# A two-layer transformer program in float32 on one core: the routed feed-forward block makes its queries and keys with the weights stationary, in one float32 product per chunk, and splits only its value and output weights

## The chip, the cores and the metric

The program runs on one core of one Trainium2 chip. The number that counts is the device time of the whole program, in microseconds (us); the median of three runs stands for the kernel. The profile is one more execution, taken by the hardware profiler.

## The reference, cut to what matters

Two layers over 2048 tokens of 512 features. The second layer's feed-forward part is "routed": 256 tokens are chosen by a score, and only these go through a small transformer block of their own. Here `x` holds the chosen tokens, 16 query heads share 8 key heads, and a head has 128 features.

```python
h = _rms_norm(x, ln1_w)
q  = (h @ wq + bq).reshape(S, 16, 128)        # S = 256
kk = (h @ wk + bk).reshape(S, 8, 128)
v  = (h @ wv + bv).reshape(S, 8, 128)
q  = q * cos + _rotate_half(q) * sin          # cos, sin: by the token's position
kk = kk * cos + _rotate_half(kk) * sin
att = softmax(causal(einsum('shd,thd->hst', q, repeat(kk)) / sqrt(128)))
x1 = x + einsum('hst,thd->shd', att, repeat(v)).reshape(S, 2048) @ wo
h2 = _rms_norm(x1, ln2_w)
mlp = silu(h2 @ w_gate) * (h2 @ w_up) @ w_down
```

## The kernel before, in words

The kernel is a chain of stages. Each stage is one block in which every engine has an instruction list of its own; engines meet at semaphores, and a stage begins only when all engines have left the one before. The names: PE is TensorE, DVE VectorE, ACT ScalarE, POOL GpSimd, SP the queue that issues most DMAs. Two stages matter here.

**stage_output1** (L2274) closes the attention of the second layer: 16 tiles of 128 tokens in 4 blocks, `out = r + (o * z) @ w`. For blocks 1 to 3 the DVE multiplies the raw attention output by the inverse sums (`normal`, L2399), ACT rounds the product to the short float format (`high`, L2360), the DVE takes the rest (`low`, L2403), and PE multiplies with three products for each chunk: high by high, high by rest, rest by high (`mm3`, L68 to L76). Such a triple stands for one product of full precision. SP loads the inverse sums `z`; the load for block 3 (`inverses(3)`) stands in SP's list behind residual loads that wait for stores of tiles 0 to 3. In the same stage POOL gathers the chosen tokens and their rows of the cosine and sine tables, and the chosen tokens are normalised, turned by PE (`transposed`) and weighed into `hT`, features by tokens. Beside this, the first 12 pieces of the query, key and value weights (128x512 each, named by `qkv_piece`) are split: ACT makes the high part (L2369), POOL the rest (L2351). At the end ACT and DVE split `hT` into `hTh` and `hTl` (L2380, L2424).

**stage_routed** (L2472) is the block of the reference above. Its first part works in 12 units of 128 tokens by 512 features (4 heads): PE makes the product with the tokens stationary (`product`, 12 matmuls), the DVE adds the bias out of the bank (`biased`, L2891), POOL multiplies by the cosines (`cosines`, L2581), the DVE by the sines in two halves (`sines`, L2901), the DVE adds the two (`turned_sum`, L2909), PE turns the four heads (`transposes`, L2645) and ACT copies them to `qT` or `kT` (L2764). Four units of values follow (L2928). Between these the remaining 20 weight pieces are split by ACT with POOL (L2588) or the DVE (L2914). Then come the scores, softmax and values of each of 16 heads (L2662 to L2688; `spread` is the turning of the probabilities at L2677), with two heads of scores issued ahead. POOL splits the output weights alone, 16 pieces, each a cast (L2604) and a subtraction (L2606). The product with `wo` takes 16 triples for each of 2 token tiles; the gated part follows.

Where a tile lies is given by hand: the weights in one large tensor `WA`, their rest parts written over them (`WAr`), the high parts in four ring buffers, and many later tiles over earlier ones.

Of the kernel before, what the change touches and what calls it, by code (L numbers as in the profile page):

```python
# [17 lines left out]
P = 128  # L18
F32 = mybir.dt.float32
# [2191 lines left out]
class Routed:  # L2211
# [4 lines left out]
    def __init__(self, G, M):  # L2216
# [5 lines left out]
        self.hTl = G.nc.alloc_sbuf_tensor_at("hTl", [P, NC, SEL], F32R, offset=self.hT_at)  # L2222
        self.hTh = G.nc.alloc_sbuf_tensor_at("hTh", [P, NC, SEL], F32R, offset=G.out_o1_at)
# [7 lines left out]
        M.sb("aligned", [P, 24])  # L2231
        self.sq_done, self.ms_done, self.sd_done, self.hn_done, self.hT_mm, self.hT_done, self.ln_in = (
            G.sem("ro_" + n) for n in ("sq", "ms", "sd", "hn", "hT_mm", "hT", "ln_in"))
        self.b_in = [G.sem(f"ro_b_in{k}") for k in range(3)]
        self.kh_done, self.kl_pool, self.kl_dve, self.hTh_done, self.hTl_done = (
            G.sem("ro_" + n) for n in ("kh", "kl_pool", "kl_dve", "hTh", "hTl"))

    def load_bias(self, queue, I, k):
        FQ, FK = NHQ * HDF, NHK * HDF
        a, name, n = ((FQ, "bk", FK), (0, "bq", FQ), (FQ + FK, "bv", FK))[k]  # L2240
        queue.dma_start(self.bias[:, a:a + n], I[name].partition_broadcast(P)).then_inc(self.b_in[k], 16)
# [32 lines left out]
def stage_output1(nc, G, I, S, R, out):  # L2274
# [12 lines left out]
    with ExitStack() as stack:  # L2287
# [15 lines left out]
        def _(sp):  # L2303
# [34 lines left out]
            R.load_bias(sp, I, 0)  # L2338

        @block.gpsimd  # L2340
        def _(pool):
            for m in range(NS):
                where = bass.IndirectOffsetOnAxis(G.idx[:, m:m + 1], 0)
                pool.indirect_dma_start(R.xs[:, m, :], None, S.xn, where).then_inc(gath, 16)
                for n, name in enumerate(("cos128", "sin128")):
                    pool.indirect_dma_start(R.cs[n][:, m, :], None, I[name], where).then_inc(gath, 16)
                pool.indirect_dma_start(R.sc[:, m:m + 1], None, S.score.unsqueeze(1), where).then_inc(gath, 16)
            for p in range(AHEAD * NC):
                whole, hi, low_part = qkv_piece(G, R, p)
                pool.wait_ge(R.kh_done, p + 1)  # L2350
                pool.tensor_tensor(low_part, whole, raw(hi), ALU.subtract).then_inc(R.kl_pool, 1)  # L2351
            pool.wait_ge(gath, 16 * 4 * NS)

        @block.scalar
        def _(act):
# [6 lines left out]
            def qkv_high(p):  # L2362

                if p == 0:
                    act.wait_ge(G.wqkv_in, 48)
                if p == NC:
                    act.wait_ge(o_mm, BT)
                whole, hi, low_part = qkv_piece(G, R, p)
                act.activation(hi, whole, ACT.Copy).then_inc(R.kh_done, 1)  # L2369

            for t in range(NT):
# [5 lines left out]
                elif k == BT - 1:  # L2377
                    for m in range(NS):
                        act.wait_ge(R.hT_done, m + 1)
                        act.activation(R.hTh[:, :, m * P:(m + 1) * P], R.hT[:, :, m * P:(m + 1) * P], ACT.Copy  # L2380
                                       ).then_inc(R.hTh_done, 1)
# [8 lines left out]
        def _(dve):  # L2390
# [30 lines left out]
            for m in range(NS):  # L2421
                dve.wait_ge(R.hTh_done, m + 1)
                cols = slice(m * P, (m + 1) * P)
                dve.tensor_tensor(R.hTl[:, :, cols], R.hT[:, :, cols], raw(R.hTh[:, :, cols]), ALU.subtract  # L2424
                                  ).then_inc(R.hTl_done, 1)
# [31 lines left out]
QU, KU = NHQ * HDF // BANK, NHK * HDF // BANK  # L2457
GROUPS = [("k", u) for u in range(KU)] + [("q", u) for u in range(QU)] + [("v", u) for u in range(KU)]
AHEAD = 3
POOL_LOWS = 26  # L2460


def qkv_piece(G, R, p):

    n, c = divmod(p, NC)
    name, u = GROUPS[n]
    cols = slice(u * BANK, (u + 1) * BANK)
    whole, low = (dict(zip("qkv", routed_qkv(WA)))[name][:, c, cols] for WA in (G.WA, G.WAr))
    return whole, R.ring[n % 4][:, c, :], low


def stage_routed(nc, G, I, R, out):  # L2472


    names = ("qk_mm", "qb", "t1", "s1", "y", "yt_mm", "yt", "v_mm", "v", "link")
    qk_mm, qb_done, t1_done, s1_done, y_done, yt_mm, yt_done, v_mm, v_done, link = (G.sem("ro_" + n) for n in names)
    b_in = R.b_in
# [3 lines left out]
    names = ("woh", "wol", "oh", "ol", "x1t_mm", "hh", "hl", "square", "rs", "guh", "gul", "gu_mm", "sig", "sg", "m", "mt_mm",  # L2481
             "mh", "ml", "wdh", "wdh_act", "wdl", "dn_mm", "dx", "delta", "added")
    (woh_done, wol_done, oh_done, ol_done, x1t_mm, hh_done, hl_done, sq_done, rs_done, guh_done, gul_done, gu_mm, sig_done,
     sg_done, m_done, mt_mm, mh_done, ml_done, wdh_pool, wdh_act, wdl_done, dn_mm, dx_done, delta_done, added) = (
        G.sem("ro_" + n) for n in names)
    wo_in, wgu_in, wd_in = ([G.sem(f"ro_{n}{k}") for k in range(4)] for n in ("wo_in", "wgu_in", "wd_in"))
    FQ, FK = NHQ * HDF, NHK * HDF
# [3 lines left out]
    NU = NS * (KU + QU)  # L2491
    JOBS = FB * NS
    scale = 1.0 / float(np.sqrt(HDF))
    with ExitStack() as stack:
        M = Memory(nc, stack, "ro_")
        WA, WAr = G.WA, G.WAr
        qT = M.far("qT", [P, NHQ, SEL])
# [8 lines left out]
        bias = R.bias  # L2506
        oT = bias[:, :].rearrange("p (h n) -> p h n", h=NHQ)
# [4 lines left out]
        three_at = nc.sbuf_base  # L2512
        qb, t1, y = (M.sb(n, [P, 2, BANK]) for n in ("qb", "t1", "y"))
        nm, ssum, rsum = (M.sb(n, [P, 3, NS]) for n in ("nm", "ssum", "rsum"))
        SB = (0, 1, 6)
        pr, pt = M.sb("pr", [P, 3, 3 * P]), M.sb("pt", [P, 2, 3 * P])
        gate = M.sb("gate", [P, NS])
        at = lambda name, shape, offset: nc.alloc_sbuf_tensor_at("ro_" + name, shape, F32R, offset=offset)
        oTh, oTl = at("oTh", [P, NHQ, SEL], qT_at), at("oTl", [P, NHQ, SEL], R.bias_at)
        mTh, mTl = at("mTh", [P, NF, SEL], qT_at), at("mTl", [P, NF, SEL], R.bias_at)  # L2520
        three = at("three", [P, 6, BANK], three_at)
        hT2h = at("hT2h", [P, NC, SEL], three_at + 2 * 2 * BANK * 4)
        sig, mt = qb, t1
        hTh, hTl = R.hTh, R.hTl
        guA = [at("guA0", [P, NC, BANK], kT_at), at("guA1", [P, NC, BANK], v_at)]
        guB = [at("guB0", [P, NC, BANK], G.out_o1_at), at("guB1", [P, NC, BANK], R.rows_at)]
        spare = [R.hTh, R.hTl]
        wo_high = [guB[1][:, h, :] for h in range(4)] + [guB[0][:, 2 + h, :] for h in range(2)]
        wo_high += [three[:, h, :] for h in range(6)]
        wo_high += [t[:, 2 * h:2 * h + 2, :].rearrange("p c n -> p (c n)") for t in spare for h in range(2)]  # L2530
        wo = [(R.ring32[h // 4][:, h % 4, :], wo_high[h], R.ring[h // 4][:, h % 4, :]) for h in range(NHQ)]

# [6 lines left out]
        def down_piece(f):  # L2539
# [7 lines left out]

        units = [(GROUPS.index((name, u)), name, off, u, m, dst) for name, off, dst, count in (("k", FQ, kT, KU), ("q", 0, qT, QU))
                 for u in range(count) for m in range(NS)]
        vunits = [(GROUPS.index(("v", u)), u, m) for u in range(KU) for m in range(NS)]  # L2550

        @block.sync
        def _(sp):
            R.load_bias(sp, I, 1)
            R.load_bias(sp, I, 2)
            for c in range(4):
                if c < 2:
# [645 lines left out]
```

## Time and profile before

| | |
|---|---|
| median of 3 runs | 1627.05 us (1625.93 to 1630.09) |
| profiled execution, its own time | 1624.44 us |
| its span, first to last instruction | 1622.7 us |
| PE busy | 1499.0 us, 92% |
| DVE, ACT, POOL busy | 1068.6, 770.7, 556.2 us |
| granted clock of TensorE, mean | 0.965 |

The span is 1.74 us shorter than the execution's own time. Matmuls are pipelined, so a matmul's listed duration is longer than the distance to the next one; distances between starts are what adds up. Where a float32 matmul of the program is run, the trace has two records for it, each with a weight load.

### The profile page before, as it was taken

The numbers are of one execution on the slowest core, as the hardware profiler recorded it, in microseconds if no ns is written. First come the engines' busy times: TensorE is split into PE (matmuls) and PEld (weight loads), VectorE is DVE, ScalarE is ACT, GpSimd is POOL, SyncE is SP. The second block draws the span as 40 slices with busy tenths as digits, with TensorE's granted clock in tenths as the row PEclk, the third lists the DMA queues.
The fourth block names the chain that finished last, engine by engine and source line by source line (L and its number), as shares of the span: only waits on it lengthen the run. The fifth ranks groups of instructions, "written<-read, shape, count | busy, mean of one in ns | idle before, by whom it ended". The sixth has DMA issues, their size and how long they took to land. (4 is left out here: it accounts for less than half of the span.)

```text
span 1622.7 us, 23648 instructions
## 1 busy us (share of the span) xinstructions
PE 1499.0 (92%) x7009; PEld 1072.6 (66%) x7009; DVE 1068.6 (66%) x2800; ACT 770.7 (47%) x1311; POOL 556.2 (34%) x752
## 2 busy tenths in 40 slices
PE   5999999999999997899788989999999987887998
PEld 4777888888767886688654545555555545666876
DVE  5453666666567577777567776666667856797583
ACT  5523666656665233333224545555554552333661
POOL 0000677777532333323111212221221224288052
PEclk9999999999999999899959999999999998998999
DMA  5002121221101234466792404314314107706121
GB/s 176 1 1 84 72 107 71 90 87 74 40 27 53 100 109 136 119 192 185 219 291 109 111 8 115 69 54 114 73 48 114 56 25 226 229 31 225 60 104 14
DMA packets 107301, 163.11 MB, mean 101 GB/s; under 512 B 12272, under 2 KB 63616, under 8 KB 100672
## 3 DMA queue, kind: packets, MB, share of 16 engines
q1 hardware_dynamic: 103200, 155.86, 31.6%
q10 hardware_dynamic: 3360, 4.72, 0.8%
q0 software_dynamic: 640, 1.31, 0.4%
q8 instruction: 47, 0.77, 0.2%
q14 instruction: 54, 0.44, 0.1%
HBM read 119.00 MB, written 42.87 MB: 100 GB/s over the span
## 5 line engine op out<-in xcount | busy, mean ns | idle before, releaser
L2042 ACT ACTIVATE l_pt<-banks 128x1024 f32<-128x1024 f32 (+3 forms) x288 | 218.5, 811 | 162.6 <-PE banks L1919 160.7
L2116 DVE CUSTOM_DVE_ANT_0 stage<-banks,l_edges 128x384 f32<-128x384 f32 (+3 forms) x384 | 201.7, 542 | 102.2 <-issue 101.1
L1956 PE MATMUL banks<-l_pt,l_v 128*64 128x512 f32 (+3 forms) x1152 | 230.8, 523 | 3.2 <-POOL l_pt L2014 3.2
L699 POOL TENSOR_TENSOR ex_hl<-ex_h,ex_hh 128x512 fp32r<-128x512 f32 x128 | 165.2, 1296 | 81.3 <-ACT ex_hh L667 81.0
L2013 POOL TENSOR_TENSOR l_turn<-l_before 128x2 f32<-128x2 f32 x192 | 39.4, 205 | 420.1 <-ACT l_pt L2042 410.5
L2119 DVE TENSOR_REDUCE l_mx<-banks 128x1 f32<-128x384 f32 (+1 forms) x208 | 113.2, 544 | 51.0 <-PE banks L1897 50.2
L732 DVE SCALAR_TENSOR_TENSOR ex_rw<-banks,ex_wb 128x512 f32<-128x512 f32 x128 | 88.3, 690 | 78.9 <-PE banks L75 78.8
L1956 PEld LDWEIGHTS banks<-l_pt,l_v 128*64 128x64 f32 x1152 | 70.3, 139 | 95.9 <-issue 71.8
L667 ACT ACTIVATE ex_hh<-ex_h 128x512 fp32r<-128x512 f32 x128 | 80.9, 632 | 103.5 <-DVE ex_h L740 102.8
L1897 PE MATMUL banks<-k,q 96*128 96x384 f32 (+3 forms) x296 | 94.9, 414 | 16.5 <-PEq L3065 8.2
L73 PE MATMUL banks<-ex_xlh,ex_wh 128*128 128x512 f32 x256 | 101.6, 397 | 2.1 <-DVE ex_rw L732 2.1
L74 PE MATMUL banks<-ex_xll,ex_wh 128*128 128x512 f32 x256 | 99.8, 390 | 0.0
L75 PE MATMUL banks<-ex_xlh,ex_wl 128*128 128x512 f32 x256 | 99.8, 390 | 0.0
L1897 PEld LDWEIGHTS banks<-k,q 96*128 96x128 f32 x296 | 54.7, 206 | 68.1 <-issue 24.2
L1897 PE MATMUL banks<-l_k,l_q 96*128 96x384 f32 (+3 forms) x296 | 89.3, 386 | 9.2 <-DVE l_mx L2116 5.5
L1897 PEld LDWEIGHTS banks<-l_k,l_q 96*128 96x128 f32 x296 | 50.6, 193 | 63.1 <-DVE l_mx L2116 26.3
L740 DVE TENSOR_TENSOR ex_h<-banks,ex_t 128x512 f32<-128x512 f32 x128 | 88.4, 691 | 1.1 <-PE banks L75 0.7
L693 POOL TENSOR_TENSOR ex_wl<-ex_ws,ex_wh 128x768 fp32r<-128x768 f32 x16 | 29.6, 1853 | 149.6 <-ACT ex_wh L655 149.6
L2014 POOL TENSOR_SCALAR_AFFINE_SELECT l_pt<-l_pt 128x256 f32<-128x256 f32 x192 | 80.7, 420 | 0.1
L661 ACT ACTIVATE ex_t<-ex_rw 128x512 f32<-128x512 f32 x128 | 79.0, 617 | 1.4 <-DVE ex_rw L732 1.4
L1919 PE MATMUL banks<-q,k 98*128 98x512 f32 (+3 forms) x288 | 68.8, 359 | 1.5 <-ACT q L2061 1.3
L1919 PE MATMUL banks<-l_q,l_k 98*128 98x512 f32 (+3 forms) x288 | 66.4, 349 | 0.7 <-ACT l_pt L2042 0.6
(463 smaller groups left out, 3647.2 us busy)
## 6 DMA issues: line engine op xcount, KB each, us to landing
ex_wb<-gates_by_expert SPq DMA_DIRECT2D x16, 1024.0 KB, 4.6
layer_v<-qkv_vs SPq DMA_DIRECT2D x16, 512.0 KB, 4.7
l_v<-layer_v SPq DMA_DIRECT2D x8, 1024.0 KB, 17.3
layer_qk<-qkv_yh SPq DMA_DIRECT2D x31, 256.0 KB, 3.2
layer_qk<-qkv_yl SPq DMA_DIRECT2D x31, 256.0 KB, 3.6
ex_ws<-ew_in SPq DMA_DIRECT2D x16, 384.0 KB, 5.0
l_q<-layer_qk SPq DMA_DIRECT2D x12, 512.0 KB, 7.7
l_k<-layer_qk SPq DMA_DIRECT2D x12, 512.0 KB, 14.1
```

Of the source, the lines that this page charges most:

```text
L73: pe.matmul(out, ah, bh, start=start and n == 0, stop=False, **kw)
L74: pe.matmul(out, ah, bl, start=False, stop=False, **kw)
L75: last = pe.matmul(out, al, bh, start=False, stop=stop and end, **kw)
L699: pool.tensor_tensor(hl[:, k % RING, :], h[:, k % RING, :], raw(hh[:, k % RING, :]), ALU.subtract).then_inc(hl_done, 1)
L732: dve.scalar_tensor_tensor(rw[:, k % 2, :], gate[k % 2][:, :], 0.0, wb[:, par, b * TB:(b + 1) * TB], ALU.max, ALU.mult).then_inc(rw_done, 1)
L740: dve.tensor_tensor(h[:, k % RING, :], up[k % 2][:, :], tt[:, k % 2, :], ALU.mult).then_inc(h_done, 1)
L1897: pe.matmul(out, q[par][0:K3, h, qt * P:(qt + 1) * P], k[par][0:K3, h, k0 * P:k1 * P], start=True, stop=True).then_inc(a_mm, 1)
L1919: last = pe.matmul(bank[:, 0:width], k[par][0:KM, h, kt * P:(kt + 1) * P], q[par][0:KM, h, qa * P:(qz + 1) * P], start=True, stop=True)
L1956: last = pe.matmul(bank[h * 2 * HD:(h + 1) * 2 * HD, (qa - b * BT) * P:(qz + 1 - b * BT) * P], v[par][:, kt, h, :], pt[:, step_part(b, j), ...
L2042: act.activation(pt[:, step_part(b, j), :, 0:width], G.banks[:, 2 * slot:2 * slot + 2, 0:width], ACT.Exp, scale=scale).then_inc(p_done, 1)
L2116: dve.tensor_tensor_reduce(cutoff[:, n % 4, 0:width], G.ps[5 + n % MB][:, 0:width], masked, 1.0, NEG, ALU.add, ALU.max, mx[:, h, m, c:c + ...
L2119: dve.reduce_max(mx[:, h, m, c:c + 1], G.ps[5 + n % MB][:, 0:width], axis=AX).then_inc(a_red, 1)
```

## The change

- Queries and keys: one matmul per chunk in plain float32, a head's 128x128 weights stationary and all 256 tokens of `hT` moving. Each head lands with features on partitions, as the scores need it; the transposes and their copies go.
- The two tables of the chosen tokens are turned once by PE and copied by ACT (`cosT`, and `sinT` with its halves exchanged).
- The rotary step is done by the DVE out of the bank: three `scalar_tensor_tensor` per head (add the bias of the partition, multiply by the table row), one of 128x256 and two of 64x256; POOL adds the two results in place.
- Weight pieces of queries and keys aren't split any more. The 8 value pieces are split inside the routed stage by ACT and POOL; nothing of this is left in stage_output1. `hT` is split in the routed stage too.
- Four value units stand after 12 of the 24 heads.
- Output weights: ACT makes all 16 high parts after the values; POOL takes rests 0 to 7 between its sums, the DVE rests 8 to 15 within the heads 4 to 11 of the attention.
- SP: `wo` is loaded at the start of the stage, `w_up` after the values, `w_gate` after the last head's product. The query and key biases come as one small tensor.
- After the attention `output_high(0)` and `(1)` stand behind `output(15)`. Several tiles lie elsewhere.

```diff
@@ stage_output1: gone @@
-            R.load_bias(sp, I, 0)
+            R.load_biases(sp, I)
-            for p in range(AHEAD * NC):
-                whole, hi, low_part = qkv_piece(G, R, p)
-                pool.wait_ge(R.kh_done, p + 1)
-                pool.tensor_tensor(low_part, whole, raw(hi), ALU.subtract).then_inc(R.kl_pool, 1)
-                if t < NC:
-                    qkv_high(t)
-                elif t > BT and t - 1 < AHEAD * NC:
-                    qkv_high(t - 1)
-                elif k == BT - 1:
-                    for m in range(NS):
-                        act.wait_ge(R.hT_done, m + 1)
-                        act.activation(R.hTh[:, :, m * P:(m + 1) * P], ...)
...
@@ stage_routed, SP @@
+            for c in range(4):
                 sp.dma_start(R.ring32[c][:, :, :], I["wo"]...).then_inc(wo_in[c], 16)
+            for w, name in ((1, "w_up"), (0, "w_gate")):
+                if w == 1:
+                    sp.wait_ge(v_mm, len(vunits))
+                else:
+                    sp.wait_ge(qk_mm, NH)
...
@@ GpSimd @@
+            def turned_sum(n):
+                dst = head(n)[1]
+                pool.wait_ge(turn_done, n + 1)
+                pool.tensor_tensor(dst, dst, t1[:, n % 3, :], ALU.add).then_inc(y_done, 1)
+            for n in range(NH):
+                turned_sum(n)
+                if n < VALUES_AT and n % 3 < 2:
+                    value_low(2 * (n // 3) + n % 3)
+                if n >= VALUES_AT + 3 and n % 3 < 2:
+                    output_low(2 * ((n - VALUES_AT) // 3 - 1) + n % 3)
+            for h in range(6, 8):
+                output_low(h)
...
@@ TensorE @@
+            def product(n):
+                w, _, h = head(n)
+                wait(pe, turn_done, n - 3)
                 for c in range(NC):
+                    last = pe.matmul(G.ps[n % 4][:, 0:SEL], w[:, c, h * HDF:(h + 1) * HDF], hT[:, c, :], start=c == 0, stop=c == NC - 1)
+                last.then_inc(qk_mm, 1)
+            for k in range(2):
+                for m in range(NS):
+                    last = pe.transpose(G.ps[6 + k][:, m * P:(m + 1) * P], cs[k][:, m, :], G.ident[:, :])
+                last.then_inc(tab_mm, 1)
+            pe.wait_ge(G.wqkv_in, 48)
+            pe.wait_ge(R.hT_done, NS)
+            for n in range(NH):
+                if n == VALUES_AT:
+                    for i in range(len(vunits)):
+                        values(i)
+                product(n)
             def scores(h):
+                if h < 2:
+                    pe.wait_ge(turn_done, NH)
+                    pe.wait_ge(tab_done, 3)
+                pe.wait_ge(y_done, NHK + h + 1)
...
@@ VectorE @@
+            def turned(n):
+                _, dst, _ = head(n)
+                part = G.ps[n % 4][:, 0:SEL]
                 dve.wait_ge(qk_mm, n + 1)
+                wait(dve, y_done, n - 2)
+                dve.scalar_tensor_tensor(t1[:, n % 3, :], part, R.hb[:, n:n + 1], cosT[:, :], ALU.add, ALU.mult)
                 for k in range(2):
+                    rows = slice((1 - k) * P // 2, (2 - k) * P // 2)
+                    last = dve.scalar_tensor_tensor(dst[k * P // 2:(k + 1) * P // 2, :], part[rows, :], R.hb[rows, n:n + 1],
+                                                    sinT[rows, :], ALU.add, ALU.mult)
+                last.then_inc(turn_done, 1)
                 if h + 2 < NHQ:
                     maxima(h + 2)
+                if 4 <= h < 12:
+                    weight_low(h + 4)
```

## Rows read from the trace of the kernel before

**Rows 1.** Windows: stretches in us, busy time (count) by engine, clock, DMA share, GB/s.

```profile
1415.20:1481.60 66.40, 54.17 (x240) 41.00 (x240) 57.05 (x58) 18.82 (x33) 53.44 (x40) 0.97 0.21 72
1481.60:1519.30 37.70, 33.70 (x208) 28.11 (x209) 28.43 (x98) 27.56 (x99) 17.98 (x19) 0.91 0.69 252
1519.30:1622.70 103.40, 94.28 (x424) 75.82 (x424) 59.10 (x82) 43.05 (x80) 33.60 (x26) 0.98 0.15 46
```

**Rows 2.** Waits, 1414 to 1482 us: total, times, longest.

```profile
PE banks L2645 <- DVE ro_y L2909: 11.3, 10, 3.1
```

**Rows 3.** Groups by line, 1414 to 1482 us: busy us, mean ns, idle.

```profile
L2588 POOL TENSOR_TENSOR WAr<-WA,ringr 128x512 fp32r<-128x512 f32 x14 | 20.7, 1492 | 0.0
```

**Rows 4.** Single lines: duration min/median/max in ns, first and last start.

```profile
L2891 DVE TENSOR_TENSOR ro_qb<-banks,bias x12: 676/678/692, 1418.3 to 1465.2; 128x512 f32<-128x512 f32 x12
...
L2901 DVE TENSOR_TENSOR ro_y<-ro_qb,routed_sin x24: 410/1504/1524, 1419.0 to 1467.8; 128x256 f32<-128x256 f32 x24
```

**Rows 5.** Timeline of stage_output1: start, duration, instruction, idle time before it.

```profile
1389.69 0.69 DVE L2399 TENSOR_TENSOR o_o<-o_z,o_o 128x512 f32<-128x512 f32 x1 [3.41 <-DMA o_z<-layer_inverse_sums]
...
1391.64 1.30 POOL L2351 TENSOR_TENSOR WAr<-WA,ringr 128x512 fp32r<-128x512 f32 x1 [4.22 <-ACT ringr L2369]
1391.69 1.80 DVE L2399 TENSOR_TENSOR o_o<-o_z,o_o 128x512 f32<-128x512 f32 x1
...
1401.13 0.80 PE L73 MATMUL banks<-out_wh,o_oh 128*128 128x512 f32 x1 [2.12 <-DVE o_ol L2403]
...
1402.15 0.63 PE L75 MATMUL banks<-out_wh,o_ol 128*128 128x512 f32 x1
1402.57 0.63 PE L73 MATMUL banks<-out_wh,o_oh 128*128 128x512 f32 x1
```

**Rows 6.** The same view, where the two stages meet.

```profile
1412.43 0.40 PE L75 MATMUL banks<-out_wh,o_ol 128*128 128x512 f32 x1
...
1413.47 1.28 DVE L2424 TENSOR_TENSOR hTl<-hT,hTh 128x512 fp32r<-128x512 f32 x2
1413.59 0.34 ACTq L2387 DMA_DIRECT2D out<-rows  x1
...
1415.22 0.47 PE L73 MATMUL banks<-ringr,hTh 128*128 128x512 f32 x1 [2.40 <-PEq L2287]
```

**Rows 7.** Timeline of PE: a value unit's last 9 products.

```profile
1478.50 0.40 PE L73 MATMUL banks<-ringr,hTh 128*128 128x512 f32 x1
...
1480.38 0.39 PE L75 MATMUL banks<-ringr,hTl 128*128 128x512 f32 x1
```

**Rows 8.** The chain that ended last, in time order, 1493 to 1515 us: start, us.

```profile
1495.72 0.43 PE banks L2686 x2
...
1502.51 0.49 PE banks L2667 x2
```

**Rows 9.** Timeline: DVE and POOL together, then 16 chained DVE subtractions.

```profile
1562.52 1.09 POOL L2614 CAST WAr<-ringf 128x512 fp32r<-128x512 f32 x1
1563.06 0.74 DVE L2984 SCALAR_TENSOR_TENSOR ro_qb<-banks,rs,ro_qb 128x512 f32<-128x512 f32 x1
...
1518.74 5.68 DVE L2951 TENSOR_TENSOR ro_oTl<-bias,ro_oTh 128x256 fp32r<-128x256 f32 x16 [2.01 <-ACT ro_oTh L2802]
```

**Rows 10.** Timeline of the attention: PE's turnings of probabilities, and DVE's pace.

```profile
1487.31 0.90 PE L2677 MATMUL banks<-ident,ro_pr 128*128 128x128 f32 x3 [2.86 <-DVE ro_pr L2946]
...
1497.20 0.55 PE L2677 MATMUL banks<-ident,ro_pr 128*128 128x128 f32 x3
...
1508.41 0.50 PE L2677 MATMUL banks<-ident,ro_pr 128*128 128x128 f32 x3
...
1510.23 0.54 PE L2677 MATMUL banks<-ident,ro_pr 128*128 128x128 f32 x3
...
1485.12 1.27 DVE L2939 TENSOR_SCALAR ro_nm<-ro_nm 128x2 f32<-128x2 f32 x1
...
1508.62 0.62 DVE L2935 TENSOR_REDUCE ro_nm<-banks 128x1 f32<-128x128 f32 x2 [0.30 <-PE banks L2669]
```

More of the change, by code:

```diff
@@ L2420, in _ @@
                     low(b + 1, k)
[L2421 to L2425, printed above, removed]
         @block.tensor
@@ L2533, in gu_piece, with head @@
+        def head(n):
+            name, h = HEADS[n]
+            return (wk, kT[:, h, :], h) if name == "k" else (wq, qT[:, h, :], h)
         def gu_piece(fb, n):
@@ L2641, in transposes @@
-            def transposes(n):
-                pe.wait_ge(y_done, n + 1)
-                wait(pe, yt_done, n - 1)
-                for j in range(HB):
-                    last = pe.transpose(G.ps[2 + n % 2][:, j * P:(j + 1) * P], y[:, n % 2, j * P:(j + 1) * P], G.ident[:, :])
-                last.then_inc(yt_mm, 1)
-            for n, (g, name, off, u, m, dst) in enumerate(units):
-                if n < NS:
-                    pe.wait_ge(R.hTl_done, m + 1)
-                wait(pe, qb_done, n - 1)
-                product(G.ps[n % 2], g, m).then_inc(qk_mm, 1)
-                if n >= 2:
-                    transposes(n - 2)
@@ L2655, in _, with values @@
-            for n, (g, u, m) in enumerate(vunits):
-                wait(pe, v_done, n - 1)
-                product(G.ps[4 + n % 2], g, m).then_inc(v_mm, 1)
-                if n < 2:
-                    transposes(NU - 2 + n)
+                    last = pe.matmul(G.ps[n % 4][:, 0:SEL], w[:, c, h * HDF:(h + 1) * HDF], hT[:, c, :], start=c == 0, stop=c == NC - 1)
+                last.then_inc(qk_mm, 1)
+            def values(n):
+                u, m = vunits[n]
+                rows = slice(m * P, (m + 1) * P)
+                wait(pe, v_done, n - 1)
+                if n == 0:
+                    pe.wait_ge(hTl_done, NS)
+                for c in range(NC):
+                    if m == 0:
+                        pe.wait_ge(vwl_done, u * NC + c + 1)
+                    _, hi, low = value_piece(u * NC + c)
+                    last = mm3(pe, G.ps[4 + n % 2], [((hTh[:, c, rows], hTl[:, c, rows]), (hi, low))], start=c == 0, stop=c == NC - 1)
+                last.then_inc(v_mm, 1)
@@ L2707, in _ @@
                     rows = slice(m * P, (m + 1) * P)
-                    last = mm3(pe, G.ps[m], [((oTh[:, h, rows], oTl[:, h, rows]), (hi, low))], start=h == 0, stop=h == NHQ - 1)
+                    last = mm3(pe, G.ps[m], [((oTh[h // 8][:, h % 8, rows], oTl[:, h, rows]), (hi, low))],
+                               start=h == 0, stop=h == NHQ - 1)
                     if h == NHQ - 1:
@@ L2745, in down @@
                     _, hi, low = down_piece(f)
-                    last = mm3(pe, G.ps[4 + m], [((mTh[:, f, rows], mTl[:, f, rows]), (hi, low))], start=f == 0, stop=f == NF - 1)
+                    last = mm3(pe, G.ps[4 + m], [((mTh[:, f, rows], mTl[f // 8][:, f % 8, rows]), (hi, low))], start=f == 0, stop=f == NF - 1)
                 return last
@@ L2811, in _ @@
                     output(h - 1)
-            output_high(0)
-            output_high(1)
             output(NHQ - 1)
-            for h in range(2, NHQ):
+            for h in range(NHQ):
                 output_high(h)
@@ L2931, in maxima, with weight_low @@
+            def weight_low(h):
+                whole, hi, low = wo[h]
+                dve.wait_ge(woh_done, h + 1)
+                dve.tensor_tensor(low, whole, raw(hi), ALU.subtract).then_inc(wol_dve, 1)
             def maxima(h):
```

274 lines of the change are left out of this document (101 added, 173 removed).

## The prediction

> **What bounds the kernel now.** I read the page first: 1622.7 us of span with PE busy for 92% of it, so most of the program is PE's. The change touches three stretches, and I cut the end of the span at them [rows 1]. In the first part of the routed stage (66.40 us) PE is busy for 54.17 us, but the DVE for 57.05 and POOL for 53.44: three engines share the limit. The waits name the holder: PE sits idle for 11.3 us before the transposes of L2645, each time until the DVE's sum is there [rows 2]. The DVE's line in [rows 4] shows the pace: twelve units from 1418.3 to 1465.2 us, so 46.9 / 11 = 4.26 us a unit, while PE's own work in a unit is 12 products at 0.235 us (1480.38 - 1478.50 = 1.88 us over eight distances [rows 7]) = 2.82 us, and four transposes at about 0.13 us (0.50 us for three, ends included [rows 10]). What makes the DVE slow is the sine step: of 128x256 elements, it takes 0.41 us at best and 1.50 us in the median [rows 4]. It reads two SBUF tensors while POOL works.
>
> The same collision stands in the stage before. There `normal` takes 0.69 us when POOL is idle, and 1.80 us when POOL's subtraction of 1.30 us has begun 0.05 us earlier [rows 5]. Three of the four groups of block 3 have it, one of them in the rows (3 times 1.1 us), and PE waits on this chain: 2.12 us before the block's last group at 1401.13 us, after which products come 0.42 us apart (1402.57 - 1402.15), the distance at TensorE's lower level of 1.2 GHz [rows 5].
>
> So the questions are: what float32 products cost PE, whether the DVE and POOL keep up, and what the earlier stage gives back.
>
> **The change, part by part.** Sums are made on the profiled execution.
>
> *A, stage_output1.* The 12 splits leave. The split pieces themselves weren't waited for; they lock the DVE. In block 3, three collisions of 1.80 - 0.69 = 1.11 us go: 3.3 us. With the last wait about 1 us shorter the clock need not drop: 8 products at 0.42 instead of 0.235 us, 1.5 us. The end of the block: PE's last product starts at 1412.43 us and ends its chain near 1412.83, the next stage's first starts at 1415.22, with the split of `hT` between (1413.47, 1.28 us) [rows 6]. Without it the block ends with the addition (about 0.7 us), a store issue (0.34 us) and the meeting of the engines (1415.22 - 1414.75 = 0.47 us): 1.5 instead of 2.4 us, 0.9 us gained. Blocks 1 and 2 lose five collisions too, but block 3 starts on the landing of its inverse sums (the DVE idle for 3.41 us until the DMA [rows 5]). That load stands behind stores which the first chain sets, so it can start up to 3.3 us earlier, or not, where the DMA queues are full. I count 0 for it. A = 5.7 us; bounds 0.9 (the DMA sets everything) and 9.
>
> *B, queries, keys, values.* PE: 24 heads of 4 float32 matmuls. The nearest row is the product with the values, of the same shape, two records of 128x256 in 0.43 us; the score product takes 0.49, where it stands next to bfloat16 masks [rows 8]. Here like follows like, so I take 0.43: 96 x 0.43 = 41.3 us (at 0.49: 47.0). That its rests vanish is why PE gains nothing: before, the same was 12 x (2.82 + 0.52) = 40.1 us. The values are unchanged: 48 x 0.235 = 11.3 us. The table transposes: 4, about 0.6 us. The stage then ends with a rotary step, of which nothing lies beside PE work: three DVE operations.
>
> What do those cost? Not shown before for this size. From above: 0.74 us, the same operation and kinds of operand with 512 elements, and that while POOL's cast (1562.52 to 1563.61) ran beside it: it wasn't locked out. From below: 5.68 / 16 = 0.355 us, a two-input operation of 256 elements in a chain [rows 9]. I take 0.40, nearest to the lower one, since the length is the same: 1.2 us a head against PE's 1.72. At 0.74 it would be 2.22, and the DVE would set the pace (24 x 2.22 = 53.3 us, 12 us more). The 64-partition halves are counted as whole ones.
>
> POOL: per three heads, three additions of 256 elements and two rests. A rest takes 1.30 us alone [rows 5], 1.49 beside others [rows 3]; the addition lies between about 0.4 (a third of that) and 1.3; by half the length and a fixed part I take 0.75. That is 3 x 0.75 + 2 x 1.3 = 4.9 us against 5.2 on PE: it just keeps up, and a lag of two heads is allowed by the three buffers. At 1.3 it would be 6.5 us for three, up to 8 us over the stage. ACT has two tables, `hT`, 8 and then 16 high parts, under 20 us in 53. The start: tables, `hT` split and first rotary step take about 5 us, while PE can fill four banks (7 us): hidden. Without those banks it would cost 3.
>
> B: before 66.4; after 0.6 + 41.3 + 11.3 + 1.5 (last rotary step and its signals) = 54.7. Gain 11.7; bounds 6.0 (0.49) and 0 (DVE at 0.74) below, 12.5 above.
>
> *C, attention.* POOL was busy with `wo` for 17.98 of 37.7 us [rows 1]. The scaling of two numbers took 1.27 us at 1485.12, and PE waited 2.86 us for its first turning at 1487.31; then at low clock and beside POOL the next four heads took 1497.20 - 1487.31 = 9.89 us, where two late ones are 1.82 apart [rows 10]. With POOL done early: the first turning about 1.5 us sooner, and four heads at 1.83 = 7.3, 2.6 us saved. Against it: the DVE gets 8 rests, one a head, some 0.6 us each in a chain. A late head has 0.30 us of DVE idle time [rows 10], so each costs 0.3: 8 x 0.3 = 2.4 us. `output_high(0)` now stands behind the last `output`: 0.65 us before PE's first product with `wo`. POOL's last two rests reach 3 us into the attention; half a microsecond is in the first term. C = 1.5 + 2.6 - 2.4 - 0.65 = 1.0 us; from -3 (clock still drops) to +3.
>
> *D, the loads.* `wo` (4 MB) now lands at the stage's start, where the queues carry 72 GB/s [rows 1] and its first reader comes after the values. `w_up` and `w_gate` come earlier than before; their first reader is behind the attention. The two bias loads stand at the end of SP's list in the stage before, with some 5 us to land. All nothing, hidden by 21 us of products at least. If the weights came late, gate-up would wait, but it has 35 us. After the attention (103.4 us, PE busy for 94.28 [rows 1]) the order of work is the same: 0.
>
> Sum: 5.7 + 11.7 + 1.0 = 18.4 us. Span 1622.7 - 18.4 = 1604.3, own time 1606.0. The profiled execution is 2.6 us below the median of the three runs, so for the median: 1627.05 - 18.4 = 1608.6 us.
>
> **The rivals.**
>
> *R1, the stage before gives nothing.* The DMA queues set block 3 and its stores. For it: [rows 5]'s wait for the inverse sums. Against: after its landing eleven more microseconds pass in which the DVE is busy for nearly all and PE waits for it. Gain 0.9 + 11.7 + 1.0 = 13.6: 1613.5 us. Chance 0.15.
>
> *R2, PE isn't the bound of the new products, or they are dearer.* Products at 0.49 us give 1614.3; DVE operations at 0.74 give 1620.3; a lagging POOL lies between. For: POOL's margin is 6%. Chance 0.17, centre 1615.
>
> *R3, slower: the lock hits the rotary step.* The new operation reads the bank, an SBUF table and an SBUF bias scalar. If the lock took it too, it would wait out POOL's work, up to 4.9 / 3 = 1.6 us a head: 1.2 + 1.6 = 2.8 us, 24 x 2.8 = 67 us instead of 41, 26 us lost: 1634.6 us. It decides from 1.72 + 18.4 / 24 = 2.5 us a head on. Against it: the row with the same kinds of operand, 0.74 us beside POOL's cast [rows 9], and L2891, never above 0.69 us beside POOL [rows 4]. Chance 0.04.
>
> The Trainium skill (SBUF — State Buffer, section "SBUF: two separate sides") says that the port pair is an exclusive lock: a DVE operation with two SBUF inputs and a GpSimd operation block each other for a whole instruction. By that rule the 1.80 us are explained, and the trace agrees (0.69 alone, 1.30 for POOL's); whether a scalar counts as the second input it doesn't say there. If it did, the time would be R3's.
>
> *R4, no change:* the gain of B is eaten by a wait I don't see. Chance 0.04.
>
> **How the numbers follow.** My forecast (1602 to 1612 us) has 0.60. With R1 and R2 the gain runs from 6 to 25 us; leaving out R3 and R4 and the outer tails of R2, the range is 1601 to 1619 us. About 0.3% (5 us) is what a measurement of this kernel tells from no change. R1, R2 and the forecast are all faster by more: 0.92. Within 0.3%: 0.04. Slower: 0.04.
>
> **What would show it.** Score products should begin some 17 us earlier than 1481.6 us. The routed stage's first product: at 1409.5 us. `normal` in block 3: four times 0.69 us. Float32 records in heads: pairs every 0.43 us, no idle time on PE from first product to last; if PE waits on the rotary step, R2 or R3. DVE operations of 0.4 to 0.5 us; above 1 us means R3. POOL's additions at 0.75 us. In the attention, heads 5 to 12 at 2.1 us apart and the others at 1.83. The prediction is wrong if the float32 products run apart by more than 0.5 us, or the clock drops within them, or block 3's inverse sums land later.

## The result and the profile after

The changed kernel took 1606.28 us (median of 4 runs, 1604.26 to 1607.17) against 1626.88 us of the kernel before (4 runs, 1625.93 to 1630.09): a ratio of 0.9868, 95% interval 0.9851 to 0.9885, so faster by 20.6 us. Predicted were 1608.6 us within 1601 to 1619. Run again later, it gave 1606.40 us and 0.9882 (0.986 to 0.9904). The profiled execution took 1604.26 us with a span of 1602.6: 20.1 us less than the 1622.7 before.

The same windows as in [rows 1], with the end of stage_output1 ahead of them (stretch in us, its length, busy time and count of PE, PEld, DVE, ACT and POOL, granted clock, DMA share, GB/s):

```profile
1352.58:1407.71 55.13, 49.86 (x201) 38.82 (x201) 31.30 (x49) 9.07 (x14) 7.86 (x8) 0.93 0.85 269
1407.71:1462.32 54.61, 52.99 (x245) 45.80 (x245) 38.77 (x78) 16.16 (x30) 33.04 (x37) 1.00 0.46 160
1462.32:1498.93 36.61, 32.00 (x209) 25.96 (x209) 28.17 (x106) 27.04 (x100) 3.51 (x4) 1.00 0.31 115
1498.93:1602.60 103.67, 94.00 (x424) 75.82 (x424) 58.90 (x82) 42.78 (x80) 33.71 (x26) 0.98 0.16 46
```

Against [rows 1], the routed stage's first part is 66.40 - 54.61 = 11.8 us shorter, the attention 37.70 - 36.61 = 1.1, the rest 0.3 longer. What remains, 7.5 us, was gained ahead of it: the routed stage begins at 1407.71 us instead of 1415.22. In the first part PE is now busy for all but 1.62 us, the wait at its end, at the full clock of 2.4 GHz. By busy time no other engine is near it (the DVE 38.77 of 54.61 us), but within the heads the DVE is closer than that, as the rows below and kernels 10 and 11 show.

Groups of that part (busy us, mean ns of one | idle time before them and what ended it):

```profile
L2591 PE MATMUL banks<-hT,WA 128*128 128x256 f32 x192 | 41.8, 379 | 0.0
L2856 DVE SCALAR_TENSOR_TENSOR ro_qT<-banks,hb,ro_sinT 64x256 f32<-64x256 f32 x32 | 15.5, 483 | 0.5
L2853 DVE SCALAR_TENSOR_TENSOR ro_t<-banks,hb,ro_cosT 128x256 f32<-128x256 f32 x24 | 11.6, 483 | 5.4 <-PE banks L2591 5.2
L2544 POOL TENSOR_TENSOR ro_qT<-ro_qT,ro_t 128x256 f32<-128x256 f32 x15 | 11.0, 732 | 16.3 <-DVE ro_qT L2856 16.3
```

PE never stands idle before a product of the heads. The DVE's idle time before the cosine step was ended by PE, and POOL's by the DVE: a pipeline with PE in front. The timeline of the DVE (start, duration, instruction, idle time before it) shows two of the 24 heads:

```profile
1457.28 0.48 DVE L2853 SCALAR_TENSOR_TENSOR ro_t<-banks,hb,ro_cosT 128x256 f32<-128x256 f32 x1 [0.25 <-PE banks L2591]
1457.78 0.98 DVE L2856 SCALAR_TENSOR_TENSOR ro_qT<-banks,hb,ro_sinT 64x256 f32<-64x256 f32 x2
1459.01 0.48 DVE L2853 SCALAR_TENSOR_TENSOR ro_t<-banks,hb,ro_cosT 128x256 f32<-128x256 f32 x1 [0.25 <-PE banks L2591]
1459.51 0.98 DVE L2856 SCALAR_TENSOR_TENSOR ro_qT<-banks,hb,ro_sinT 64x256 f32<-64x256 f32 x2
```

A head takes 1459.01 - 1457.28 = 1.73 us, four pairs of records at 0.43. The DVE's three operations of 0.48 us fill 1.48 us of it with the gaps between them, and it waits 0.25 us for the next bank.

Block 3 in stage_output1, to be held against [rows 5], and the junction, against [rows 6]:

```profile
1387.13 0.69 DVE L2372 TENSOR_TENSOR o_o<-o_z,o_o 128x512 f32<-128x512 f32 x1 [3.19 <-DMA o_z<-layer_inverse_sums]
1388.66 0.69 DVE L2391 TENSOR_TENSOR rows<-banks,rows 128x512 f32<-128x512 f32 x1 [0.84 <-DMA rows<-layer_residual]
...
1393.86 0.69 DVE L2372 TENSOR_TENSOR o_o<-o_z,o_o 128x512 f32<-128x512 f32 x1
...
1395.99 0.50 PE L73 MATMUL banks<-out_wh,o_oh 128*128 128x512 f32 x1 [0.63 <-DVE o_ol L2376]
...
1405.74 0.40 PE L75 MATMUL banks<-out_wh,o_ol 128*128 128x512 f32 x1
...
1407.71 0.41 PE L2609 MATMUL banks<-ident,routed_cos 128*128 128x128 f32 x2 [1.57 <-PEq L2282]
```

All twelve `normal` operations of the stage take 0.68 to 0.69 us. From block 3's first one to PE's last group it is 1395.99 - 1387.13 = 8.86 us (11.44 before), from there to the last product 9.75 (11.30 before), and over the junction 1.97 (2.79 before): 2.58 + 1.55 + 0.82 = 4.95 us. The other 2.56 us of the 7.5 were there already: block 3's inverse sums had been used at 1389.69 us before, now at 1387.13.

### The profile page after: what moved, and what is told of

Its sections match the earlier page's. It is cut to its first block and busy times, and to the rows that moved or that the text cites. A ratio compares the mean times of both kernels' runs of the same rounds, so it can differ in the third digit from the quotient of the medians.

```text
span 1602.6 us, 23599 instructions
## 1 busy us (share of the span) xinstructions
PE 1492.9 (93%) x7013; PEld 1072.9 (67%) x7013; DVE 1038.3 (65%) x2826; ACT 759.8 (47%) x1294; POOL 505.4 (32%) x722
## 5 line engine op out<-in xcount | busy, mean ns | idle before, releaser
L1897 PE MATMUL banks<-k,q 96*128 96x384 f32 (+3 forms) x296 | 94.9, 414 | 16.6 <-PEq L3019 8.3
```

The source lines that it names most:

```text
L1897: pe.matmul(out, q[par][0:K3, h, qt * P:(qt + 1) * P], k[par][0:K3, h, k0 * P:k1 * P], start=True, stop=True).then_inc(a_mm, 1)
```

## The experiments

Each kernel ran beside the kernel before on the same chip: before took 1624.97 us beside kernels 1 to 4, 1626.11 beside 5, 6, 7 and 9, and 1623.69 beside 8, 10, 11 and the second run of 6. The changed kernel itself ran beside the second group alone (kernel 5), so the others are held against it by their ratios. Since the landing of a load shifts a whole execution by some microseconds, I read stretches of the trace too: **S**, from the first product of stage_output1, behind a wait of 3.48 us in every profile, to the table transposes (before, where these don't exist, to the routed stage's first product: 1415.22 - 1352.37 = 62.85 us; changed kernel 55.13 and, in its second profile, 55.53), and **T**, from the transposes to the first product with `wo` (91.22 and 91.24 us in the changed kernel).

**1. The splits back in stage_output1 (e1_pool_back).** To the changed kernel the 12 old splits are added in place; their results aren't used.

```diff
+            for p in range(12):
+                whole, hi = old_piece(p)
+                pool.wait_ge(x_hi, p + 1)
+                pool.tensor_tensor(hi, whole, raw(hi), ALU.subtract).then_inc(x_lo, 1)
...
+                if t < NC:
+                    old_high(t)
+                elif t > BT and t - 1 < 12:
+                    old_high(t - 1)
```

> The changed kernel with the twelve splits of the stage before put back in their old places: ACT makes the high parts, POOL subtracts, in place over the high part; nothing reads the result, the weights themselves stay as they are. Theory (the stage before gained because POOL's subtractions no longer lock the DVE): the multiplication by the inverse sums takes about 1.8 us again in three groups of block 3, PE's wait before the last group comes back, and the time is 5 to 7 us above the changed kernel's, 1611 to 1613 us. Rival (the gain comes from the split of hT leaving the end of the stage, or from the DMA): 0 to 1 us above.

Measured: 1610.17 us, 0.9906 (0.989 to 0.9922). By the ratios that is 4 to 6 us above the changed kernel. S is 62.46 us, about 7 more; T is 91.21. The collision is back in the timeline:

```profile
1391.11 1.44 POOL L2354 TENSOR_TENSOR ringr<-WA,ringr 128x512 fp32r<-128x512 f32 x1 [3.91 <-ACT ringr L2371]
1391.31 1.80 DVE L2396 TENSOR_TENSOR o_o<-o_z,o_o 128x512 f32<-128x512 f32 x1
```

The DVE's operation starts 0.20 us after POOL's and takes 1.80 us. All three collisions of block 3 are back (1.80, 1.81, 1.80 us), and with them PE's wait of 2.14 us before the last group and the products 0.42 us apart behind it: 11.33 us from there to the last product, as in the kernel before (11.30).

**2. ACT's half of them alone (e2_act_only).** As 1, without POOL's subtractions.

```diff
-            for p in range(12):
-                whole, hi = old_piece(p)
-                pool.wait_ge(x_hi, p + 1)
-                pool.tensor_tensor(hi, whole, raw(hi), ALU.subtract).then_inc(x_lo, 1)
```

> The same with only ACT's twelve high parts put back, none of POOL's subtractions. Theory (the lock): nothing changes in the DVE's multiplications, 0.69 us each; ACT's 0.6 us a piece stand behind the high part that PE needs, so 0 to 1 us above the changed kernel, 1606 to 1607 us. Rival (ACT's queue was what PE waited for): most of the 5 to 7 us come back here already.

Measured: 1605.07 us, 0.9881 (0.9862 to 0.99), S 55.51, T 91.21: no different from the changed kernel. ACT's copies cost this stage nothing. The stage's gain comes from POOL's subtractions, but for the 0.82 us at the junction, which kernel 1 keeps (1.97 us there too).

**3. The rotary step from SBUF (e3_turn_from_sbuf).** ACT copies each head out of its bank into a buffer of three, and the same three DVE operations read that; ACT's splits are strewn between the copies.

```diff
-                part = G.ps[n % 4][:, 0:SEL]
-                dve.wait_ge(qk_mm, n + 1)
+                part = qc[:, n % 3, :]
+                dve.wait_ge(qc_done, n + 1)
```

> The changed kernel, but ACT copies each head out of the bank to SBUF and the rotary step reads the copy, so that its three operations have two SBUF tensors and an SBUF scalar. ACT's value and output splits are spread between the copies. Theory (the forecast's: what kept the rotary step out of the lock was that it reads the bank): operations of 0.5 us alone but above 1 us beside POOL, a head takes about 1.3 us of DVE and up to 1.6 us of POOL one after the other, 2.9 us, and the part with the 24 heads grows from 54.6 to 75 to 82 us, 1626 to 1634 us in all. Rival (the lock doesn't matter for operations this short): the heads stay at 1.73 us and the time at 1606 to 1608 us.

Measured: 1626.22 us, 1.0008 (0.9995 to 1.0022): the whole gain is gone. The groups of its first part (columns as above), and its window:

```profile
L2865 DVE SCALAR_TENSOR_TENSOR ro_qT<-ro_qc,hb,ro_sinT 64x256 f32<-64x256 f32 x32 | 27.0, 842 | 0.5
L2547 POOL TENSOR_TENSOR ro_qT<-ro_qT,ro_t 128x256 f32<-128x256 f32 x15 | 13.3, 885 | 21.5 <-DVE ro_qT L2865 21.5
```

```profile
1406.56:1478.70 72.14, 56.37 (x244) 46.21 (x245) 60.51 (x78) 25.12 (x54) 41.23 (x37) 0.95 0.45 159
```

With both inputs in SBUF the sine halves rise from 483 to 842 ns in the mean, and POOL's additions from 732 to 885. Two rivals are a slower read from SBUF as such, and a DVE that waits for ACT's copies. The DVE's first two pairs of sine halves, and what POOL does beside the second, speak against the first:

```profile
1410.59 0.97 DVE L2865 SCALAR_TENSOR_TENSOR ro_kT<-ro_qc,hb,ro_sinT 64x256 f32<-64x256 f32 x2
1412.09 2.26 DVE L2865 SCALAR_TENSOR_TENSOR ro_kT<-ro_qc,hb,ro_sinT 64x256 f32<-64x256 f32 x2
...
1411.65 1.01 POOL L2547 TENSOR_TENSOR ro_kT<-ro_kT,ro_t 128x256 f32<-128x256 f32 x1 [49.95 <-DVE ro_kT L2865]
1412.62 1.45 POOL L2552 TENSOR_TENSOR WAr<-WA,ro_guB 128x512 fp32r<-128x512 f32 x1
```

Before POOL begins, the pair takes 0.97 us, against 0.98 from the bank; beside POOL's addition and rest it takes 2.26. And the DVE waited for ACT's copies for 1.7 us in all. Without the transposes (0.46 us) and the values (about 11.3, in part at the lower clock) some 60 us are left for 24 heads, 2.5 us a head: the point which R3 named as the one where the gain is gone. The heads with both of POOL's operations beside them take 2.8 us, those with the addition alone 1.9. So the lock is real for the rotary step too, and what keeps the changed kernel out of it is that the large operand comes from a bank. The Trainium skill (SBUF — State Buffer, section "SBUF: two separate sides") says that a DVE operation with two SBUF inputs and a GpSimd one that reads SBUF exclude each other, and leaves open whether a scalar read from SBUF is such an input. By the 483 ns beside a POOL that is busy for 33.04 of 54.61 us it is not; with the 0.97 and 2.26 us above the trace agrees with the rule.

**4. The rests of `wo` late (e4_rests_late).** The DVE's eight rests stand behind the 16 `output_low` instead of one in each of heads 4 to 11.

```diff
-                if 4 <= h < 12:
-                    weight_low(h + 4)
...
+            for h in range(8, NHQ):
+                weight_low(h)
```

> The changed kernel with the DVE's eight rests of the output weights taken out of the attention and put behind the sixteen subtractions that follow it. Theory (in the heads with a rest the DVE sets the pace at 2.13 us, and PE's own 1.83 us would without): heads 5 to 12 at 1.83 us, attention 2.4 us shorter; PE reaches the ninth chunk of the output product 11 us after the first, the rests are there after 10.5 us, so nothing is lost: 1603.9 us. Rival (it is given back in the product with the output weights): no change, 1606.3 us, with PE waiting before the ninth chunk.

Measured: 1602.66 us, 0.9859 (0.9843 to 0.9874). T is 88.57 us, 2.65 less than in the changed kernel, and no wait appears before the products that read these rests.

**5. The changed kernel again (after_again).**

> The changed kernel as it is, so that the next kernels stand beside it on one chip. Both theories: 0.987 of the kernel before, about 1605 us. The first product of the routed stage should again come near 1408 us of the span, give or take the landing of the third block's inverse sums, and the scores 54.6 us after the table transposes.

Measured: 1606.40 us, 0.9882 (0.986 to 0.9904); T 91.24, S 55.53.

**6. Number 4, and ACT's first two high parts ahead (e5_both, e5_again).** `output_high(0)` and `(1)` go ahead of `output(15)`, whose wait for PE they needn't share.

```diff
             act.wait_ge(s_mm, NHQ)
+            output_high(0)
+            output_high(1)
             output(NHQ - 1)
-            for h in range(NHQ):
+            for h in range(2, NHQ):
                 output_high(h)
```

> The rests of wo moved behind the output_low copies (as in the run before), and ScalarE's first two copies of the attention outputs' high parts ahead of the wait for the last output. My account: the rests give 2.1 to 2.7 us (heads 5 to 12 back to 1.8 us each), and the wait before the first product of the output projection falls from 1.72 to about 1.0 us, together 2.8 to 3.4 us under the changed kernel beside it, near 1602. Rival: what the attention gives comes back as waits for the loads of the gate and up weights in the last part, then no gain over the changed kernel. The order of ScalarE's copies alone is worth 0.7 us, so it is shown by the trace and not by the time.

> The kernel with the rests of wo and ScalarE's first two high parts moved, once more, beside the next kernels: about 0.985 of the kernel before, and from the table transposes to the first product of the output projection 87.7 us, against 91.2 of the changed kernel.

Measured: 1601.83 us, 0.9856 (0.9832 to 0.9881), beside 1606.40 for the changed kernel; and again 1602.14 us, 0.9865 (0.9843 to 0.9887). T is 87.74 us in both profiles, 3.5 less than the changed kernel's. The timeline of PE, two of the turnings that were held up by a rest before, and the first product with `wo`:

```profile
1482.84 0.50 PE L2639 MATMUL banks<-ident,ro_pr 128*128 128x128 f32 x3
1484.65 0.54 PE L2639 MATMUL banks<-ident,ro_pr 128*128 128x128 f32 x3
...
1497.40 0.47 PE L73 MATMUL banks<-ro_woA,ro_oTh 128*128 128x512 f32 x1 [0.48 <-DVE ro_oTl L2906]
```

The wait is 0.48 us, in the changed kernel 1.33. By the ratios the kernel is 3 to 4 us better than the changed one; the intervals overlap, so it is the stretch, alike in two profiles, that shows the 3.5 us.

**7. Block 3's loads ahead of four residual rows (e9_inverses_first).**

```diff
+            values(3)
+            inverses(3)
             for t in range(BT, 2 * BT):
                 residual(t)
-            values(3)
-            inverses(3)
```

> SyncE's queue alone: in the last stage of the first output, the values and inverse sums of block 3 are issued ahead of the residual rows 4 to 7. It asks what the earlier start of block 3 hangs on, which I had counted at nothing and which gave 2.6 us of the change. Theory: SyncE stands at residual(4) to (7) until rows are stored, so the inverse sums of block 3 come late; issued ahead, block 3's product with them starts where TensorE is free and the stage ends 1 to 3 us earlier, the time 1 to 3 us under the changed kernel. Rival 1: the transfer's own landing is late whatever its issue, because the queues are full, then within 0.5 us. Rival 2: the residual rows then come late instead and block 2 waits for them, then slower by up to 3 us.

Measured: 1613.39 us, 0.993 (0.9903 to 0.9956), 7.0 us slower than the changed kernel beside it. S is 63.55. The DVE, in the timeline:

```profile
1386.31 0.69 DVE L2391 TENSOR_TENSOR rows<-banks,rows 128x512 f32<-128x512 f32 x1 [9.54 <-DMA rows<-layer_residual]
```

Rival 2: the block's inverse sums are no longer waited for at all, but residual row 4, issued at 1371.1 us behind 2 MB, isn't used until 1386.31. The loss is more than twice the 3 us that rival 2 allowed.

**8. The same by half (e10_two_rows_first, on kernel 6).** Rows 4 and 5, then values and inverse sums of block 3, then the other rows.

```diff
+            residual(4)
+            residual(5)
             values(3)
             inverses(3)
-            for t in range(2 * BT, NT):
+            for t in range(6, NT):
                 residual(t)
```

> The kernel with the rests of wo and ScalarE's first two high parts moved, and SyncE's queue changed by less than in the run before: residual rows 4 and 5, then values and inverse sums of block 3, then rows 6 and 7. Account from the run before: there VectorE stood 9.5 us at residual row 4, behind 2 MB of block 3. With two rows ahead that wait should go, and either block 3 starts 1 to 2 us earlier and the time is 1 to 2 us under the kernel beside it, or row 6 comes late in place of row 4 and it is slower by 1 to 5 us. I take the second as likelier, since the transfer of values and inverse sums takes over 5 us and the rows are wanted every 2 us.

Measured: 1609.57 us, 0.9909 (0.9884 to 0.9934), 7.4 us slower than kernel 6. S is 63.01; now the DVE waits two rows later:

```profile
1383.32 0.69 DVE L2391 TENSOR_TENSOR rows<-banks,rows 128x512 f32<-128x512 f32 x1 [7.21 <-DMA rows<-layer_residual]
```

Block 3's first `normal` starts 38.0 us after the start of S, and 40.6 us in kernel 7, against 34.6 to 36.8 in the kernels with the old order. With a DMA share of 0.85 in this stage, as the first window above shows, neither order that I tried lets block 3 start earlier.

**9. The gate and up weights late (e8_late_loads).** `w_up` and `w_gate` as before, after the last product of the heads.

```diff
-                if w == 1:
-                    sp.wait_ge(v_mm, len(vunits))
-                else:
-                    sp.wait_ge(qk_mm, NH)
...
+            sp.wait_ge(qk_mm, NH)
```

> One part of the change undone: the gate and up weights are loaded as before, after the last query or key product, in the old order, instead of the up weights after the values and the gate weights after the products. I counted this part at 0: the waits in the gate and up stage should stay under 0.3 us in all and the time within 0.3% of the changed kernel. Rival: the later start leaves TensorE waiting for the first feed-forward block, then some us slower, and the part from the output projection to the end is longer than 103.7 us.

Measured: 1605.81 us, 0.9877 (0.9852 to 0.9901), T 91.22: no effect.

**10. A fourth operation for each head (e6_four_ops).** The cosine product is written once more, into a tile that nothing reads.

```diff
+                dve.scalar_tensor_tensor(ex[:, n % 3, :], part, R.hb[:, n:n + 1], cosT[:, :], ALU.add, ALU.mult)
```

> The changed kernel with a fourth VectorE operation for each query and key head, which repeats the cosine product into a tile that nothing reads. It asks how far the rotary step is from setting the pace of the 24 heads: TensorE takes 1.73 us a head, VectorE 1.5. Theory: each operation is 0.50 us, four are 2.0 us a head, and the 24 heads take 48.0 us instead of 41.6: 6 us slower, near 1612. Rival: the operations are 0.40 us and only 0.48 when they wait for TensorE's banks, so four fit into 1.73 and the time stays within 1 us.

Measured: 1608.36 us, 0.9905 (0.9878 to 0.9932). T is 95.45 us, 4.2 more than in the changed kernel. A head of the DVE, and PE's first scores:

```profile
1457.29 0.48 DVE L2854 SCALAR_TENSOR_TENSOR ro_t<-banks,hb,ro_cosT 128x256 f32<-128x256 f32 x1
1457.69 0.47 DVE L2855 SCALAR_TENSOR_TENSOR ro_extra<-banks,hb,ro_cosT 128x256 f32<-128x256 f32 x1
1458.18 0.98 DVE L2858 SCALAR_TENSOR_TENSOR ro_qT<-banks,hb,ro_sinT 64x256 f32<-64x256 f32 x2
1459.19 0.48 DVE L2854 SCALAR_TENSOR_TENSOR ro_t<-banks,hb,ro_cosT 128x256 f32<-128x256 f32 x1
```

```profile
1464.96 0.77 PE L2630 MATMUL banks<-ro_kT,ro_qT 128*128 128x128 f32 x2 [3.93 <-issue]
```

The DVE has no idle time left within the heads and takes 1.90 us a head, not 2.0: the repeated operation starts 0.40 us after the first. From the transposes to the scores it is 57.54 us, 2.9 more than in the changed kernel, and not 24 x (1.90 - 1.73) = 4.1. In the twelve heads ahead of the values PE isn't held up: their 96 records take 20.89 us in both kernels, since PE may run ahead by the banks. During the values the DVE catches up, at the price of some 0.6 us of PE. Only in the twelve heads behind them does the DVE's lag last to the end: from its first operation there to the scores it is 1464.96 - 1442.08 = 22.9 us (12 x 1.90 = 22.8), against 1462.32 - 1441.74 = 20.6 in the changed kernel. So the DVE sets the length of the last twelve heads, and PE that of the first. The other 1.3 us of T are the attention's (37.91 us at a clock of 0.92, against 36.61 at 1.00): after 3.93 us of waiting, PE's first score products take 0.77 us instead of 0.46.

**11. Three of four chunks (e7_three_chunks).** Every query and key product leaves out the last chunk, a quarter of its sum.

```diff
-                for c in range(NC):
-                    last = pe.matmul(..., start=c == 0, stop=c == NC - 1)
+                for c in range(NC - 1):
+                    last = pe.matmul(..., start=c == 0, stop=c == NC - 2)
```

> The changed kernel with the last of the four chunks of hT left out of every query and key product, so these outputs are wrong in value: TensorE's work for a head falls from 1.73 to 1.30 us. If TensorE alone set the pace the 24 heads would take 31.2 us, 10.4 less. Theory: VectorE's three operations at 0.50 us then set it, 36.0 us, and the gain is 5.5 us. Rival: GpSimd's four additions and splits for each head, up to 4.9 us for three heads, set it at 1.64 us a head, and the gain is 2.2 us.

Measured: 1601.2 us (1595.58 to 1603.71), 0.9863 (0.9837 to 0.989). The times scatter too much to say what it gained; the profile, of the fastest run, says it: 47.69 us from the transposes to the scores, 6.9 less than the changed kernel (PE alone would have given 10.4), and T 5.4 less (PE waits 3.99 us before the scores, and the attention again starts at a lower clock). Two heads of the DVE:

```profile
1445.93 0.48 DVE L2853 SCALAR_TENSOR_TENSOR ro_t<-banks,hb,ro_cosT 128x256 f32<-128x256 f32 x1
...
1447.44 0.49 DVE L2853 SCALAR_TENSOR_TENSOR ro_t<-banks,hb,ro_cosT 128x256 f32<-128x256 f32 x1
```

They are 1.51 us apart with nothing idle. From the DVE's first operation behind the values to the scores it is 1452.05 - 1433.85 = 18.2 us, and 12 x 1.51 = 18.1: here too the DVE sets the last twelve heads. PE's 72 records ahead of the values take 16.74 us, near to its own 12 x 1.30 = 15.6. POOL's rival pace of 1.64 us a head (12 x 1.64 = 19.7 us) isn't there.

## Why the prediction was right, and which terms were off

The forecast had the right mechanism in each part. Of 18.4 us predicted for the span, 20.1 came. The medians moved by 20.6 us, and by 19.7 beside the second run; with the mean S of the ten profiles below, the stretches make 19.4. So about 1 us of the first number is the luck of these executions.

**A, stage_output1: predicted 5.7 us, came 7.5.** This is the term that was mis-sized. Its three counted parts were 3.3 + 1.5 + 0.9 and came as 2.6 + 1.5 + 0.8; the first is short because block 3's first group waited 0.84 us for its residual row. What I had counted at 0 is the earlier start of block 3 ("it can start up to 3.3 us earlier, or not"). It gave 2.6 us in this profile. Measured from the start of the stage's products, block 3 starts at 37.3 and 37.6 us in the two profiled kernels that hold POOL's subtractions (before and kernel 1), and in the ten profiles without them, whose loads in this stage stand in the old order, at 34.6 to 36.8, in the mean 35.75. So some 1.7 us of it are the change's, and about 1 us is the luck of this execution. S says the same as a whole: 62.85 and 62.46 with the subtractions, 55.1 to 57.0 without, in the mean 55.9, a gain of 6.8 us. Block 3's start varied by 2.3 us among those ten. Kernels 1 and 2 show that POOL's subtractions are the cause and ACT's copies aren't. Why the load can start earlier is seen in SyncE's queue, whose issues of block 3's inverse sums stand here before and in the changed kernel:

```profile
1377.78 2.37 SPq L1667 DMA_DIRECT2D o_z<-layer_inverse_sums  x4
...
1376.03 1.96 SPq L1667 DMA_DIRECT2D o_z<-layer_inverse_sums  x4
```

From the end of this issue to the use it is 9.0 to 9.5 us in all twelve profiles, with the subtractions or without, so the use follows the issue. Counted from the start of S, the issue ends at 27.8 and 28.4 us with the subtractions and at 25.4 to 27.6 (mean 26.6) without. In the queue it stands behind residual loads that wait for the stores of tiles 0 to 3; tile 3's store is issued at 20.1 us before and at 20.5 in kernel 1, but at 16.6 in the changed kernel. The store comes 3.5 us earlier and the load 2: how the full DMA queues share out the difference isn't shown.

R1, that the DMA sets everything here, falls. But the DMA isn't idle cover either: kernels 7 and 8 moved block 3's loads ahead and lost 7 us each.

**B, queries, keys and values: predicted 11.7, came 11.8.** The 24 heads took 24 x 1.73 = 41.5 us (41.3), from the last product to the scores it took 1.62 (1.5). The DVE's operations were priced at 0.40 us and took 0.48, 0.50 apart, inside the bounds and with nothing lost, since PE needs 1.73 us a head. Kernels 10 and 11 set the two engines against each other from both sides: the DVE's own pace is 1.51 us a head (in the changed kernel too, where it starts late and catches up, its first six heads start 1.51 us apart), so PE is the slower by 0.22 us. The margin is thinner than the 0.5 us that I had reckoned with. R2's price for a slow DVE, 24 times the excess, is of the wrong form: kernel 10's excess of 0.17 us a head cost 2.9 us and not 4.1, since the first twelve heads hide most of theirs. POOL's addition took 0.73 us (0.75), its rests 1.28. R2 falls with these numbers, and R3 with kernel 3, which is what R3 describes, at the price of 17.5 us in this part.

**C, attention: predicted 1.0, came 1.1**, term by term: first turning 4.24 us after the scores' start instead of 5.71, 1.5 (1.5); the next four heads in 6.98 us instead of 9.89, 2.9 (2.6), at the full clock; eight rests at about 0.33 us, -2.6 (-2.4); the wait before `wo`, -0.85 (-0.65). Kernels 4 and 6 confirm the two losses by giving both back: 2.65 and 0.85 us. The two turnings' rows:

```profile
1466.56 0.55 PE L2639 MATMUL banks<-ident,ro_pr 128*128 128x128 f32 x3 [1.43 <-DVE ro_pr L2898]
...
1473.54 0.50 PE L2639 MATMUL banks<-ident,ro_pr 128*128 128x128 f32 x3
```

**D, loads and the rest: predicted 0, came -0.3**, and kernel 9 shows that the order of the gate and up loads has no part in it.

## What to carry to other kernels

When work leaves an engine that locks another one, look beyond the collisions in the last block: each one in an earlier block also holds up the stores and with them the next loads, so count that gain by the shift of the chain that releases them, not with zero (here 1.7 of at most 3.3 us). Where GpSimd works beside VectorE, an operand that stays in its bank is worth more than a buffer that frees the bank sooner: the copy through SBUF cost all that the change had gained. And a margin between two engines is read well by adding one operation and by taking some away; but ask where the lag can be made up: the twelve heads ahead of the values hid most of it, and only the twelve before the scores came out as heads times the slower pace, both times within 0.1 us.

## What the hardware showed that I had not expected

The same VectorE operation from a bank (128x256, float32) starts 0.40 us after an equal one on the same data, but 0.50 us where the next one reads other partitions or another bank, with 0.47 to 0.48 us recorded for each. I had taken 0.40 for all; why they differ stays open.

PE's first score products took 0.77 us instead of 0.46, and the attention ran at a granted clock of 0.92 or 0.93, after waits of 3.93, 3.99 and 8.86 us (kernels 10, 11 and 3); after 1.62 us in the changed kernel the clock stayed at 1.00. Each of the three attentions was 37.9 to 38.1 us long instead of 36.6. Ahead of a dense stage a wait of 4 us thus came with a further 1.3 to 1.5 us behind it. Between 1.62 and 3.93 us nothing was tried at this place; but in stage_output1 a wait of 2.12 us shortly behind one of 1.03 had products 0.42 us apart behind it (the kernel before), and so had one of 2.14 behind one of 0.88 (kernel 1).
